# A one-core MoE and gated recurrence kernel: where its first zero stores, weight roundings, rank work and transposing loads stand

## The chip, the cores and the metric

The kernel runs on one core of a Trainium2 chip. The metric is the device time of one execution in microseconds (us). Three executions of the kernel before took 873.31, 873.27 and 871.41 us; their median is 873.27 us.

## The reference

The input `x` has 32 sequences of 256 tokens with 256 channels. Two layers follow each other, each with a residual sum:

```python
x = x + moe(x, cond, ...)              # shared expert + 2 of 8 routed experts per token
x = x + recurrence(cond, x, W, b, a)   # 256 steps over the tokens of a sequence
# moe, for every token:
shared = silu(xf @ w1) * (xf @ w3) @ w2
s = sigmoid(concat(xf, tf) @ router_W);  top 2 of s + router_bias;  gates = s_sel / sum(s_sel)
h = gelu(xf @ W1e[e]);  y = h @ W2e[e];  routed = sum of gate * y over the two experts
out = (shared + routed) / 3
# recurrence, for every step t:
gate = sigmoid(h @ Wh.T + z_t @ Wz.T + b);  h = tanh(h * (1 - alpha) + gate * z_t)
```

## The kernel before

Every float32 operand of a large product is split into two float16 parts, high and low, and three products (high by high, low by high, high by low) are summed. The split of a weight is called its rounding here. It takes one ScalarE operation (the high part, L1168) and one VectorE operation (the low part, L1482) on 128x1024 elements. `CONV` (L731 to L735) lists the eleven weight pieces in order: numbers 0 and 1 are w1 and w3, 2 is w2, 3 to 6 are the first expert matrices (w1e), 7 to 10 the second (w2e). `CONV_SLOT` says at which unit a piece is rounded; -1 is before the first unit. The pieces pass through four staging buffers, so the load of piece n waits until piece n-4 is rounded (L820).

The 8192 tokens are 64 tiles of 128 and lie in six sections of 8, 8, 12, 12, 12 and 12 tiles. A group is four tiles. A section passes through these steps:

- `load_x` (L795) loads a group of tokens on SP's queue. `x_high` on ScalarE and `low_x` on VectorE (L1020, L1213) split them into `x_parts`. `turn_x` (L807) then turns the group into `xs` with four transposing DMAs on SP's queue (L814).
- LOGITS: TensorE multiplies `xs` with the router weights. VectorE finds the two experts of each token in two parts of `route`. RANKS: TensorE counts the tokens of each expert. VectorE works out the slot of each token in `place`, again in two parts.
- `scatter` (L958) writes each tile twice into `x_slots` in device memory, one indirect DMA for each of its two experts, on GpSimd's queue. Slots that no token takes must hold zeros, so `clear_slots` (L932) stores zeros over all slots beforehand: 3 MB for the first section, 3 MB for the second, and later 1 MB each for the rows that the longer sections add.
- `load_pair` (L828) brings two tiles of slots back, turned, as `xe` (L834, SP's queue). There are four buffers for it.
- An expert unit computes the up product of one pair and the down product of the pair two units earlier. ScalarE evicts the result into `y_pair` (three buffers, L1055) and SP stores it (L851). `gather` (L971) fetches the two results of each token (L983, GpSimd's queue) and VectorE adds them with the gates (`gated`).
- A shared unit computes a part of the shared expert for one group.

The program is a list of 152 units in a fixed order. Section 0 has 8 shared units (0 to 7) and then 12 expert units (8 to 19). Section 1 has 12 expert units (20 to 31) and 8 shared units (32 to 39). Each later section has 16 expert units and 12 shared units. The 256 steps of the recurrence stand from unit 34 on, at places written out by hand in tables. Each engine has a function `body(u)`, and each walks through the same units in the same order. Each of the engines, and SP with its DMA issues, executes strictly in order. GpSimd starts what it has at unit u when the up products of the unit before have ended (L993).

`PREP_UNIT` gives the unit in which a group is split and turned: before, groups 2 and 3 at -1, groups 4, 5 and 6 (section 2) at 14, 16 and 18. `LOGITS_UNIT` was -3, 2, 21 for the first three sections, and RANKS came 3 units later for section 0 and 4 units later for the others. `SCATTER_AT` gives the units of the scatters: 2 to 6, 9 to 14 and 28 to 34 for the first three sections. The section's first slot loads wait for all its scatters: `first_pairs(0)` stands ahead of unit 0 on SP's queue, the wait for section 1 stands in unit 16 (L870), and `first_pairs(2)` in unit 35 (L881).

Of the kernel before, what the change touches and what calls it, by code (L numbers as in the profile page):

```python
# [71 lines left out]
LOGITS_UNIT = [-3, 2] + [START[_n - 1] + 1 for _n in range(2, NS)]  # L72
# [5 lines left out]
for _n in range(NS):  # L78
    _first = LOGITS_UNIT[_n] + 7
    _end = START[_n] - 5  # L80
    SCATTER_AT.append([2 + max(_j // 2, _j - 3) if _n == 0 else _first + min(_j, _j * max(_end - _first, 1) // SECTIONS[_n]) for _j in range(SECTIONS[_n])])
    _first = FIRST_PAIR[_n] + PAIRS[_n]
    GATHER_AT.append([_first + _j + (2 if _n == 0 else 1) for _j in range(SECTIONS[_n])])
# [318 lines left out]
for _n in range(NS):  # L402
    for _u, _what in ((0, LOGITS), (3 if _n == 0 else 4, RANKS)):
# [19 lines left out]
def moe_gated_recurrence(nc, x, cond, router_w, router_b, w1, w3, w2, w1e, w2e, gate_w, gate_b, alpha, out):  # L423
# [34 lines left out]
    with ExitStack() as ctx:  # L458
# [276 lines left out]
        CONV_SLOT = [-1] * NSTAGE + [0, 1, 2, 3, 4, 5, 6]  # L735
# [58 lines left out]
        def _(sp):  # L794
# [12 lines left out]
            def turn_x(q):  # L807
# [3 lines left out]
                for i in range(2):  # L811
                    sp.wait_ge(s_xlo, 2 * q + i + 1)
                    for j in (2 * i, 2 * i + 1):
                        sp.dma_start_transpose(xs[:, q % NXS].rearrange("p h k s -> p (h k) s")[:, :, j * P:(j + 1) * P],  # L814
                                               x_parts[:, q % NXP, j].rearrange("p h c -> p (h c)")).then_inc(s_xs[q % NXP], 16)
# [39 lines left out]
            def prepare(at):  # L855
                for q in range(N_GROUPS):
                    if PREP_UNIT[q] == at:
                        turn_x(q)
                        if q + NXT < N_GROUPS:
                            load_x(q + NXT)  # L860
# [51 lines left out]
        def _(pool):  # L912
# [92 lines left out]
        def _(act):  # L1005
# [175 lines left out]
            for q in range(TILE0[1] // GROUP):  # L1181
                for i in range(2):
                    x_high(q, i)
                if q < N_ACT_LOADS:
                    src, _, a, k, w = conv_parts(CONV[q])
# [634 lines left out]
```

## Time and profile before

| what | value |
|---|---|
| median of three runs | 873.27 us |
| span of the profiled execution | 964.0 us |
| TensorE busy (matmuls) | 771.4 us, 80% of the span |
| VectorE busy | 531.1 us, 55% |
| ScalarE busy | 461.6 us, 48% |
| GpSimd busy | 272.8 us, 28% |
| HBM read, written | 39.90 MB, 55.84 MB |

The profiled execution is one run of the program under the hardware profiler. Its own time is given as its span, 964.0 us from the first to the last instruction; no other time of that execution is recorded. It is 90.7 us longer than the median of the runs without the profiler. Durations below are from the profiled execution.

### The profile page before, as it was taken

The numbers are of one execution on the slowest core, as the hardware profiler recorded it, in microseconds if no ns is written. First come the engines' busy times: TensorE is split into PE (matmuls) and PEld (weight loads), VectorE is DVE, ScalarE is ACT, GpSimd is POOL, SyncE is SP. The second block draws the span as 40 slices with busy tenths as digits, with TensorE's granted clock in tenths as the row PEclk, the third lists the DMA queues.
The fourth block names the chain that finished last, engine by engine and source line by source line (L and its number), as shares of the span: only waits on it lengthen the run. The fifth ranks groups of instructions, "written<-read, shape, count | busy, mean of one in ns | idle before, by whom it ended". The sixth has DMA issues, their size and how long they took to land.

```text
span 964.0 us, 23915 instructions
## 1 busy us (share of the span) xinstructions
PE 771.4 (80%) x8642; PEld 547.5 (57%) x8642; DVE 531.1 (55%) x1974; ACT 461.6 (48%) x1332; POOL 272.8 (28%) x286
## 2 busy tenths in 40 slices
PE   2368857777999969998886999888698999998553
PEld 1135646643587735587763558675355887465332
DVE  4546413444766436758444777644477545677444
ACT  3345523243555534565552566555255666455233
POOL 2244403655203453401325330233432000432000
PEclk9679978798989998999998999989799999999555
DMA  7985999548637432955532484753253452222001
GB/s 194 364 257 121 210 206 216 168 148 178 156 85 188 137 116 72 208 110 140 161 116 88 97 189 78 157 125 127 77 121 88 90 139 98 90 72 66 1 12 45
DMA packets 180195, 127.99 MB, mean 133 GB/s; under 512 B 132434, under 2 KB 160884, under 8 KB 180084
## 3 DMA queue, kind: packets, MB, share of 16 engines
q1 hardware_dynamic: 164420, 83.39, 36.7%
q0 software_dynamic: 14400, 41.96, 13.8%
q8 instruction: 76, 1.25, 0.6%
q10 hardware_dynamic: 1264, 1.10, 0.5%
q14 instruction: 35, 0.29, 0.1%
HBM read 39.90 MB, written 55.84 MB: 99 GB/s over the span
## 4 chain that ended last, share of the span: by engine, by line
PE 52%; DVE 17%; ACT 10%; another core or an unknown queue 7%; issue 6%; SPq 4%; DMA 3%; DVEq 0%; ACTq 0%
PE bank L1550 51%; SPq L814 3%; DVE hid_low L1335 2%; DVE pre L1384 2%; DVE taken L1381 2%; ACT th L1093 2%; DMA y_got<-in_L_cond_W1e_dram 2%; DVE o_ch L1404 2%; ACT hs_high L1101 2%; DVE r_sum L1354 1%; PE bank L1722 1%; DVE r_part L1350 1%; ACT hid_high L1046 1%; DVE hs_low L1390 1%
## 5 line engine op out<-in xcount | busy, mean ns | idle before, releaser
L1550 PE MATMUL bank<-xe,w1e_high 128*128 128x128 f16 x1360 | 223.2, 227 | 22.4 <-DMA xe<-x_slots_even 7.1
L1550 PE MATMUL bank<-xs,w_high 128*128 128x512 f16 x512 | 176.3, 392 | 21.9 <-ACT full L1062 12.8
L1093 ACT ACTIVATE th<-bank 128x64 f32<-128x64 f32 x256 | 57.3, 224 | 226.7 <-PE bank L1550 171.0
L1335 DVE TENSOR_TENSOR hid_low<-full,hid_high 128x512 f16<-128x512 f32 (+1 forms) x152 | 103.0, 677 | 105.8 <-ACT hid_high L1046 75.3
L1550 PE MATMUL bank<-xe,w1e_low 128*128 128x128 f16 x680 | 150.7, 226 | 1.7 <-issue 1.6
L1381 DVE SCALAR_TENSOR_TENSOR taken<-th,zq 128x64 f32<-128x64 f32 x256 | 57.3, 224 | 171.2 <-ACT th L1093 151.6
L1550 PEld LDWEIGHTS bank<-xe,w1e_high 128*128 x1360 | 120.9, 101 | 42.0 <-issue 27.7
L1550 PE MATMUL bank<-hs_high,gwt_high 128*128 128x32 f16 x1024 | 80.4, 180 | 76.8 <-ACT hs_high L1101 63.3
L1550 PEld LDWEIGHTS bank<-hs_high,gwt_high 128*128 128x128 f16 x1024 | 69.6, 99 | 114.3 <-ACT hs_high L1101 84.0
L1101 ACT ACTIVATE hs_high<-pre 128x64 f16<-128x64 f32 x256 | 65.6, 256 | 99.3 <-DVE pre L1384 90.8
L1550 PE MATMUL bank<-xs,w_low 128*128 128x512 f16 x256 | 100.4, 392 | 0.3 <-issue 0.3
L1390 DVE TENSOR_TENSOR hs_low<-hist,hs_high 128x64 f16<-128x64 f32 x256 | 57.1, 223 | 77.6 <-ACT hist L1102 71.2
L1550 PE MATMUL bank<-w2e_high,hid_high 128*128 x340 | 97.3, 286 | 0.6 <-issue 0.5
L1550 PE MATMUL bank<-w2e_high,hid_low 128*128 x340 | 96.4, 283 | 1.6 <-issue 1.6
L1550 PEld LDWEIGHTS bank<-xs,w_high 128*128 128x128 f16 x512 | 51.1, 100 | 80.4 <-ACT full L1062 13.3
L1550 PE MATMUL bank<-w2e_low,hid_high 128*128 x340 | 96.1, 283 | 0.4 <-issue 0.4
L983 POOL DMA_INDIRECT y_got<-y_slots_odd,where x64 | 65.4, 1021 | 91.8 <-PE bank L1550 75.6
L953 POOL TENSOR_TENSOR fence_pool<-zero 128x1 f32<-128x1 f32 x12 | 3.7, 306 | 308.9 <-DMA y_slots_odd<-y_pair 92.2
L983 POOL DMA_INDIRECT y_got<-y_slots_even,where x64 | 65.1, 1018 | 81.8 <-PE bank L1550 63.2
L1042 ACT ACTIVATE full<-bank 128x512 f32<-128x512 f32 x88 | 50.8, 578 | 67.8 <-remote 41.2
L968 POOL DMA_INDIRECT x_slots_even<-x_parts,where x64 | 68.1, 1064 | 51.5 <-PE bank L1550 32.4
L968 POOL DMA_INDIRECT x_slots_odd<-x_parts,where x64 | 64.0, 1001 | 56.1 <-PE bank L1550 36.5
(152 smaller groups left out, 1746.1 us busy)
## 6 DMA issues: line engine op xcount, KB each, us to landing
y_slots_even<-y_pair SPq DMA_DIRECT2D x41, 256.0 KB
y_slots_odd<-y_pair SPq DMA_DIRECT2D x41, 256.0 KB
x_tok<-in_x_dram SPq DMA_DIRECT2D x16, 512.0 KB
x_res<-in_x_dram SPq DMA_DIRECT2D x16, 512.0 KB
out_dram<-o_tok SPq DMA_DIRECT2D x32, 256.0 KB
x_slots_even<-zeros POOLq DMA_DIRECT2D x1, 3072.0 KB, 16.1
x_slots_odd<-zeros POOLq DMA_DIRECT2D x1, 3072.0 KB, 23.5
y_got<-in_L_cond_W1e_dram SPq DMA_DIRECT2D x4, 512.0 KB, 20.3
```

What stands on the lines that cost most here:

```text
L814: sp.dma_start_transpose(xs[:, q % NXS].rearrange("p h k s -> p (h k) s")[:, :, j * P:(j + 1) * P], x_parts[:, q % NXP, j].rearrange("p h ...
L968: pool.indirect_dma_start(x_slots[n % 2], at_slots(n, j, k), x_parts[:, q % NXP, i].rearrange("p h c -> p (h c)"), None).then_inc(s_scat[n ...
L983: pool.indirect_dma_start(y_got[:, tile % NYG, k, :], None, y_slots[n % 2][0:(2 * PAIRS[n] - 1) * P, :], at_slots(n, j, k)).then_inc(s_got ...
L1042: nc.scalar.activation(full32[:, u.i % 2, 0:hidden(u)], up_bank(u)[:, 0:hidden(u)], ACT.Gelu, scale=1.0 / UP)
L1093: nc.scalar.activation(flat3(th[:, s % 2]), gate_sums(s), ACT.Tanh, scale=0.5 / UP).then_inc(s_th, 1)
L1101: nc.scalar.activation(flat3(hs[0][:, s % 2]), src, ACT.Tanh).then_inc(s_hhi, 1)
L1335: dve.tensor_tensor(hid[1][:, u.i % NR, some], full32[:, u.i % 2, some], hid[0][:, u.i % NR, some], ALU.subtract).then_inc(s_lo, 1)
L1381: dve.scalar_tensor_tensor(flat3(taken[:, s % 2]), flat3(th[:, s % 2]), 1.0, flat3(z_of(s // HALF)[:, s % HALF]), ALU.add, ALU.mult).then_ ...
L1384: dve.tensor_tensor(flat3(pre[:, s % 2]), flat3(taken[:, s % 2]), flat3(kept[:, s % 2]), ALU.add).then_inc(s_pre, 1)
L1390: dve.tensor_tensor(flat3(hs[1][:, s % 2]), flat3(hist[:, s % TS]), flat3(hs[0][:, s % 2]), ALU.subtract).then_inc(s_hlo, 1)
L1404: ins = dve.scalar_tensor_tensor(o_ch[:, kc].rearrange("p j b t -> p t j b"), z_of(c)[:, :, kc, :].rearrange("p (t j) b -> p t j b", j=2), ...
L1550: return pe.matmul(out_ap, w, mov, start=start, stop=stop, skip_group_check=True)
```

## The change

The zero store of section 0 is issued when the second group of tokens has landed (`s_x[1]`), and no longer when the first eight transposes are done. The zero store of section 1 waits until seven pieces (three shared and all of w1e) are rounded; it stands ahead of section 0's scatters on GpSimd. The load of w2 moves from SP's queue to ScalarE's. Pieces 3 to 6 are rounded at units 1, 1, 2, 2 and no longer at -1, 0, 1, 2; pieces 7 to 10 stay at 3, 4, 5, 6. SP loads four w1e pieces before it turns group 2, and a w2e piece between groups 2 and 3. Group 3 is split at unit 0. The logits of section 1 move from unit 2 to 4 with RANKS three units later, at 7 and not at 6; those of section 2 from unit 21 to 23 with RANKS at 27 and not at 25. Section 0's last scatter moves from unit 6 to 5, section 1's scatters lie one a unit at 9 to 16 and not at 9 to 14, and section 2's at 30 to 34 and not at 28 to 34. Section 2's groups are split at units 8, 12 and 18, and their twelve transposes are issued one a unit: at 8 to 11, 12 to 15 and 18 to 21.

```diff
-LOGITS_UNIT = [-3, 2] + [START[_n - 1] + 1 for _n in range(2, NS)]
+PREP_UNIT.update({3: 0, 4: 8, 5: 12, 6: 18})
+LOGITS_UNIT = [-3, 4, 23] + [START[_n - 1] + 1 for _n in range(3, NS)]
+RANKS_AFTER = [3, 3] + [4] * (NS - 2)
...
-    _first = LOGITS_UNIT[_n] + 7
+    _first = LOGITS_UNIT[_n] + RANKS_AFTER[_n] + (2 if _n == 1 else 3)
...
-        CONV_SLOT = [-1] * NSTAGE + [0, 1, 2, 3, 4, 5, 6]
+        CONV_SLOT = [-1] * N_SHARED_CONV + [1, 1, 2, 2, 3, 4, 5, 6]
...
-            def turn_x(q):
+            def turn_tile(q, j):
                 if q >= NXS:
                     sp.wait_ge(s_up, FIRST_SHARED[q - NXS] + MID)
-                for i in range(2):
-                    sp.wait_ge(s_xlo, 2 * q + i + 1)
-                    for j in (2 * i, 2 * i + 1):
-                        sp.dma_start_transpose(...)
+                sp.wait_ge(s_xlo, 2 * q + j // 2 + 1)
+                sp.dma_start_transpose(...)
...
             def prepare(at):
-                for q in range(N_GROUPS):
-                    if PREP_UNIT[q] == at:
-                        turn_x(q)
-                        if q + NXT < N_GROUPS:
-                            load_x(q + NXT)
+                for q in range(TILE0[2] // GROUP, N_GROUPS):
+                    spread = section_of(q * GROUP) == 2
+                    for j in range(GROUP):
+                        if PREP_UNIT[q] + (j if spread else 0) == at:
+                            turn_tile(q, j)
+                            if j == GROUP - 1 and q + NXT < N_GROUPS:
+                                load_x(q + NXT)
...
-            load_weight(N_ACT_LOADS)
             for q in range(TILE0[1] // GROUP):
                 load_x(q + NXT)
-            for n in range(N_ACT_LOADS + 1, NSTAGE + 2):
+            for n in range(N_SHARED_CONV, NSTAGE + 3):
                 load_weight(n)
-            for q in range(TILE0[1] // GROUP, N_GROUPS):
-                if PREP_UNIT[q] < 0:
-                    turn_x(q)
-                    if q + NXT < N_GROUPS:
-                        load_x(q + NXT)
-            for n in range(NSTAGE + 2, len(CONV)):
+            for q in range(TILE0[1] // GROUP, TILE0[2] // GROUP):
+                turn_x(q)
+                load_weight(NSTAGE + 1 + q)
+                load_x(q + NXT)
+            for n in range(NSTAGE + 5, len(CONV)):
                 load_weight(n)
...
-            for q in range(TILE0[1] // GROUP):
-                turned(pool, q)
+            pool.wait_ge(s_x[1], 16)
             pool.wait_ge(s_zero0, 2)
             clear_slots(0, 0, 0, PAIRS[0])
+            pool.wait_ge(s_conv, N_SHARED_CONV + 4)
             clear_slots(1, 1, 0, PAIRS[1])
...
-                if q < N_ACT_LOADS:
+                for n in (q, N_ACT_LOADS) if q == N_ACT_LOADS - 1 else (q,):
```

## Rows read from the trace of the kernel before

**Rows 1.** The page of the kernel before: its span.

```profile
span 964.0 us, 23915 instructions
```

**Rows 2.** Busy time by stretch; columns are in the header line.

```profile
core 0: us, PE busy (x) PEld busy (x) DVE busy (x) ACT busy (x) POOL busy (x), PEclk, DMA share, GB/s
24.00:48.00 24.00, 7.78 (x38) 2.89 (x37) 13.40 (x43) 7.13 (x11) 4.84 (x5) 0.64 1.01 364
48.00:72.00 24.00, 15.96 (x108) 7.24 (x106) 10.32 (x44) 10.41 (x14) 11.74 (x11) 0.79 0.90 258
120.00:144.00 24.00, 12.19 (x108) 10.34 (x109) 3.71 (x6) 5.99 (x13) 0.00 (x0) 0.78 1.04 210
400.00:500.00 100.00, 89.09 (x1212) 72.25 (x1211) 59.74 (x258) 58.41 (x174) 22.90 (x23) 0.95 0.54 139
```

**Rows 3.** SP's queue, timeline: start, duration, instruction, count.

```profile
6.58 10.52 SPq L814 DMA_TRANSPOSE xs<-x_parts  x8
...
19.67 11.60 SPq L823 DMA_DIRECT2D y_got<-in_L_cond_W1e_dram  x2
```

**Rows 4.** DMA issues, microseconds to landing last: zero stores of the first 150 us.

```profile
x_slots_even<-zeros POOLq DMA_DIRECT2D x1, 3072.0 KB, 16.1
x_slots_odd<-zeros POOLq DMA_DIRECT2D x1, 1024.0 KB, 14.2
```

**Rows 5.** Waits, 20 to 50 us: who waited for whom, total, times, longest.

```profile
PE bank L1550 <- ACT full L1062: 12.8, 1, 12.8
POOL fence_pool L953 <- DVE smask L1306: 20.6, 1, 20.6
```

**Rows 6.** TensorE timeline: the logits of section 1, with the wait ahead.

```profile
56.82 0.19 PE L1550 MATMUL bank<-rwx_high,xs 128*128 128x8 f16 x2 [7.46 <-DMA xs<-x_parts]
```

**Rows 7.** VectorE timeline, 25 to 45 us.

```profile
25.24 1.22 DVE L1482 SCALAR_TENSOR_TENSOR w_low<-y_got,w_high 128x1024 f16<-128x1024 f32 x1
...
37.65 0.23 DVE L1317 COPY ranks<-bank 128x72 f32<-128x72 f32 x1
...
42.15 2.49 DVE L1213 SCALAR_TENSOR_TENSOR x_parts<-x_tok,x_parts 128x512 f16<-128x512 f32 x4
44.55 0.68 DVE L1328 SCALAR_TENSOR_TENSOR full<-full,bank 128x512 f32<-128x512 f32 x1
```

**Rows 8.** GpSimd timeline: first, ninth and last scatter of section 0.

```profile
42.44 1.33 POOL L968 DMA_INDIRECT x_slots_even<-x_parts,where  x1 [0.33 <-issue]
...
64.15 1.31 POOL L968 DMA_INDIRECT x_slots_even<-x_parts,where  x1 [9.52 <-PE bank L1550]
...
74.01 1.22 POOL L968 DMA_INDIRECT x_slots_even<-x_parts,where  x1 [0.30 <-issue]
```

**Rows 9.** ScalarE timeline: first expert unit, three late evictions, unit 21.

```profile
84.54 0.60 ACT L1042 ACTIVATE full<-bank 128x512 f32<-128x512 f32 x1 [0.58 <-PE bank L1550]
...
129.81 0.60 ACT L1055 ACTIVATE y_pair<-bank 128x512 f32<-128x512 f32 x1 [9.68 <-DMA y_slots_even<-y_pair]
...
141.34 0.60 ACT L1055 ACTIVATE y_pair<-bank 128x512 f32<-128x512 f32 x1 [7.48 <-DMA y_slots_even<-y_pair]
...
146.40 0.60 ACT L1042 ACTIVATE full<-bank 128x512 f32<-128x512 f32 x1 [2.94 <-PE bank L1550]
...
151.69 0.38 ACT L1055 ACTIVATE y_pair<-bank 128x256 f32<-128x256 f32 x1 [4.21 <-DMA y_slots_even<-y_pair]
```

**Rows 10.** Chain of waits: one undisturbed expert unit of TensorE.

```profile
105.76 3.10 PE bank L1550 x36
```

**Rows 11.** SP's queue, timeline: the three groups of section 2.

```profile
112.40 11.66 SPq L814 DMA_TRANSPOSE xs<-x_parts  x4
...
129.42 5.20 SPq L814 DMA_TRANSPOSE xs<-x_parts  x4
...
141.35 5.14 SPq L814 DMA_TRANSPOSE xs<-x_parts  x4
```

**Rows 12.** Scatters of section 2 (L968): durations in ns, first and last start.

```profile
L968 POOL DMA_INDIRECT x_slots_even<-x_parts,where x24: 966/986/1439, 181.3 to 226.3; - x24
```

More of the change, by code:

```diff
@@ L78 @@
 for _n in range(NS):
-    _first = LOGITS_UNIT[_n] + 7
+    _first = LOGITS_UNIT[_n] + RANKS_AFTER[_n] + (2 if _n == 1 else 3)
     _end = START[_n] - 5
-    SCATTER_AT.append([2 + max(_j // 2, _j - 3) if _n == 0 else _first + min(_j, _j * max(_end - _first, 1) // SECTIONS[_n]) for _j in range(SECTIONS[_n])])
+    SCATTER_AT.append([2 + _j // 2 if _n == 0 else 9 + _j if _n == 1 else _first + min(_j, _j * max(_end - _first, 1) // SECTIONS[_n]) for _j in range(SECTIONS[_n])])
     _first = FIRST_PAIR[_n] + PAIRS[_n]
@@ L402 @@
 for _n in range(NS):
-    for _u, _what in ((0, LOGITS), (3 if _n == 0 else 4, RANKS)):
+    for _u, _what in ((0, LOGITS), (RANKS_AFTER[_n], RANKS)):
         _u += LOGITS_UNIT[_n]
@@ L805, in load_res, with turn_x @@
                 sp.dma_start(x_res[:].rearrange("p j c -> p (j c)"), x_in[q]).then_inc(s_res, 16)
-            def turn_x(q):
+            def turn_tile(q, j):
                 if q >= NXS:
                     sp.wait_ge(s_up, FIRST_SHARED[q - NXS] + MID)
-                for i in range(2):
-                    sp.wait_ge(s_xlo, 2 * q + i + 1)
-                    for j in (2 * i, 2 * i + 1):
-                        sp.dma_start_transpose(xs[:, q % NXS].rearrange("p h k s -> p (h k) s")[:, :, j * P:(j + 1) * P],
-                                               x_parts[:, q % NXP, j].rearrange("p h c -> p (h c)")).then_inc(s_xs[q % NXP], 16)
+                sp.wait_ge(s_xlo, 2 * q + j // 2 + 1)
+                sp.dma_start_transpose(xs[:, q % NXS].rearrange("p h k s -> p (h k) s")[:, :, j * P:(j + 1) * P],
+                                       x_parts[:, q % NXP, j].rearrange("p h c -> p (h c)")).then_inc(s_xs[q % NXP], 16)
+            def turn_x(q):
+                for j in range(GROUP):
+                    turn_tile(q, j)
             def load_weight(n):
@@ L855, in prepare @@
             def prepare(at):
-                for q in range(N_GROUPS):
-                    if PREP_UNIT[q] == at:
-                        turn_x(q)
-                        if q + NXT < N_GROUPS:
-                            load_x(q + NXT)
+                for q in range(TILE0[2] // GROUP, N_GROUPS):
+                    spread = section_of(q * GROUP) == 2
+                    for j in range(GROUP):
+                        if PREP_UNIT[q] + (j if spread else 0) == at:
+                            turn_tile(q, j)
+                            if j == GROUP - 1 and q + NXT < N_GROUPS:
+                                load_x(q + NXT)
             def body(u):
@@ L1183, in _ @@
                     x_high(q, i)
-                if q < N_ACT_LOADS:
-                    src, _, a, k, w = conv_parts(CONV[q])
-                    act.dma_start(stage[:, q].rearrange("p (k w) -> p k w", k=k), src).then_inc(s_stage[q], 16)
+                for n in (q, N_ACT_LOADS) if q == N_ACT_LOADS - 1 else (q,):
+                    src, _, a, k, w = conv_parts(CONV[n])
+                    act.dma_start(stage[:, n].rearrange("p (k w) -> p k w", k=k), src).then_inc(s_stage[n], 16)
             for n in range(N_ACT_LOADS):
@@ L1190, in _ @@
             act_sigmoid(0)
-            for n in range(N_ACT_LOADS, NSTAGE):
+            for n in range(N_ACT_LOADS, N_SHARED_CONV):
                 conv(n)
@@ L1464, in body @@
                         route(n, 6, N_ROUTE_LINKS, gap)
-                    if n > 0 and since == 4:
+                    if n > 0 and since == RANKS_AFTER[n]:
                         place(n, 0, 5, gap)
-                    if n > 0 and since == 5:
+                    if n > 0 and since == RANKS_AFTER[n] + 1:
                         place(n, 6, N_PLACE - 1, gap)
@@ L1534, in _ @@
             route(0, 0, N_ROUTE_LINKS, lambda: None)
-            for n in range(N_ACT_LOADS, NSTAGE):
+            for n in range(N_ACT_LOADS, N_SHARED_CONV):
                 conv(n)
```

## The prediction, made before the changed kernel ran

> **What bounds the kernel now.** I read the busy time by stretch first [rows 2]. From 400 to 500 us TensorE is busy for 89.09 of 100 us, so the late stages are bound by TensorE and the change touches nothing there. The early stretches differ. TensorE is busy for 7.78 of 24 us from 24 to 48 us, for 15.96 of 24 from 48 to 72, and for 12.19 of 24 from 120 to 144 us, while the DMA engines are at 0.90 to 1.04 of their time. The units stand in one fixed order, and each unit behind a late one is late too. I therefore count an early microsecond saved as one saved at the end.
>
> Then I read who waits in these stretches. In the first, TensorE waits 12.8 us for ScalarE's silu [rows 5], and ScalarE is late because it rounds a w1e piece whose load is slow. That load runs beside the 6 MB of zero stores: DMA moves 364 GB/s there [rows 2], and SP needs 11.60 us to issue two ordinary copies [rows 3]. VectorE is behind the same rounding, so the slots of section 0 come late and GpSimd waits 20.6 us for them [rows 5]. Next TensorE waits 7.46 us for the transposes of group 3 [rows 6]. GpSimd's scatters are held too: the ninth waits 9.52 us for TensorE's pace [rows 8]. In the third stretch ScalarE cannot evict because the store of an earlier result has not landed: 9.68, 7.48 and 4.21 us [rows 9]. Those stores are behind SP's twelve transposes for section 2, issued in three blocks of 11.66, 5.20 and 5.14 us [rows 11].
>
> **Part A, the start up to the first expert unit (unit 8).** Its up product ends at 84.54 us now [rows 9]. I follow the changed order from the end of the first eight transposes, which is 6.58 + 10.52 = 17.1 us [rows 3], plus a delay D, since the first zero store now runs beside them.
>
> - *D.* The trace shows no first-stage transpose beside a zero store. The nearest rows are the four of section 2 beside the later 1 MB stores (landing 14.2 us [rows 4]): 11.66 us, or 2.92 each, where the first eight take 10.52, or 1.32 each [rows 3, 11]. Eight at that price give D = 8 x 1.60 = 12.8 us. Below, D = 0 if the issue rate holds. By bytes alone, 3 MB at 364 GB/s [rows 2] are 8.6 us of all DMA engines, part of it in time that the transposes leave free. The rows where SP is slowed by zeros [rows 3, 11] are the nearest, so I take D = 6.
> - *VectorE to the last w1e piece.* Now the rounding of w2 ends at 25.24 + 1.22 = 26.46 us [rows 7], 9.4 us after the transposes; its load comes earlier on ScalarE's queue, which can't hold it longer. Behind it place(0) takes 42.15 - 37.65 = 4.5 us, with no slow load ahead of it any more. Group 2 takes half of 2.49, or 1.25 us, and group 3 the same in unit 0. Units 0 to 2 add three products and two low parts at 0.68 us and four roundings at 1.22 [rows 7], so 3.4 + 4.9 us. The sum is 17.1 + 9.4 + 4.5 + 2.5 + 8.3 = 41.8 us, plus D.
> - *GpSimd.* The wait for seven rounded pieces is new, and all sixteen scatters of section 0 are queued behind it, with whoever reads their slots. They start near 42.5 + D, where they start at 42.44 now [rows 8]. So VectorE's earlier place(0) is worth nothing by itself. What goes is the 9.52 us wait in their middle, because TensorE is ahead by then. Fifteen steps from the first to the last scatter take 74.01 - 42.44 - 9.52 = 22.05 us. The last one is issued 0.1 + D - 9.5 = D - 9.4 us later than now.
> - *Behind them.* The first pairs are loaded only when all scatters have landed, and from the last scatter to the end of the first expert unit I keep today's distance, 84.54 - 74.01 = 10.5 us [rows 8, 9]. The second 3 MB of zeros now runs beside the scatters, the w2e loads and group 3's transposes. It is bounded by 0 and by another 8.6 us; much of that traffic has slack, so I take 2 us.
> - Moving w2's load costs ScalarE one DMA issue and takes one from SP, and the logits of section 1 at unit 4 no longer meet an unfinished group 3, so I count nothing for either. If group 3 is still late there, its wait is a part of the 2 us.
>
> A comes to 9.4 - 6 - 2 = 1.4 us gained, between 9.4 and -12.
>
> **Part B, units 8 to 21.** ScalarE starts unit 21's eviction at 146.40 us, 61.9 us behind unit 8's [rows 9]. Thirteen undisturbed units of 3.10 us [rows 10] are 40.3 us, so 21.6 us are lost. The three waits for stores are 21.4 us of it [rows 9]. The change breaks the 22.0 us of blocks [rows 11] into single transposes, 1.3 us in a unit of 3.1. What comes in their place is the zero store of 2 MB at unit 16, not 14. In SP's order the wait for section 1's scatters stands in unit 16 as well, and behind it the slot loads, the stores and four transposes of group 6. With 2.92 us for a transpose, SP needs about 6.4 us for a unit of 3.1 over the 14.2 us of the zeros [rows 4, 10, 11], so it slips by 7 to 8 us. The last scatter, issued only in unit 16, adds about 2 us. Three y_pair buffers and four slot buffers swallow a part of this, but I charge 10 of the 21.4 us and take 11 us gained. Ends: 3 us if the waits only change their place, 18 us if the buffers cover nearly all.
>
> **Part C, section 2's scatters.** GpSimd spends 24 x (0.986 + 0.30) = 30.9 us on them, from 181.3 to 226.3 us [rows 8, 12], and the gathers of section 1 are queued in between. Now they start two units later, 6.2 us [rows 10]. The stretch also holds eight gathers of about the same cost, 10 us, and spans 46.3 us, so some 5 us of it are slack. The last scatter comes 1 to 6 us later, and TensorE's residual products of section 1 wait for the gathers behind it. I take 2 us lost, between 0 and 6. The ranks and the router work are as many instructions as before and I count nothing for their new places; they are a few short VectorE operations ahead of nothing that is late.
>
> **The sum.** 1.4 + 11 - 2 = 10.4 us gained, 953.6 us against the profiled 964.0 [rows 1]. The median of the runs is 873.27, or 0.906 of the profile. Scaled by that the gain is 9.4 us, and the time is 864.
>
> **Rivals.**
>
> *The zeros do not slow the transposes.* D = 0, and the slip in part B goes too, from 10 to about 5 us. For it: in the trace sixteen of the transposes [rows 3, 11] take about 1.3 us each, beside other traffic. Against it: the rows with zeros in flight [rows 3, 11]. The gain is 7.4 + 16 - 2 = 21 us in the profile, but the start can't gain it all, since TensorE's shared units need their time; with half of the start's part, 17 us. The time is 873.3 - 15.5 = 858. The Trainium skill (DMA: Bandwidth & Descriptors, section Queues, rings and completion order) says that each DMA engine takes turns between its queue rows, a whole packet at a time, so that GpSimd's zeros could not shut SP's row out. By that rule D would be small, which is this rival. The trace speaks against it for SP's copies, with 11.60 us for issuing two [rows 3].
>
> *The zero stores hold SP, twice (slower).* D = 12.8 at the start, and the 2 MB at unit 16 now meets the slot loads on which the change from section 0 to section 1 hangs. The start is 9.4 - 12.8 - 2 = -5.4 us, B keeps 3 us, C costs 6: together 8.4 us lost, or 881 us. The point from which this decides is the first block of eight: if it takes longer than 10.5 + 9.4 = 20 us, the start loses. For it: the 2.92 us for each transpose [rows 11]. Against it: one 3 MB store may be done before the eight are.
>
> *It does not spread what matters (no change).* The late evictions wait for the landing of a store, and DMA is at 1.04 from 120 to 144 us [rows 2]. If the DMA engines and not SP's order hold the stores, spreading the issues changes nothing: B gives 3 us and C takes 2, the start 1.4, for about 871 us. Against it: the DMA load falls by the time of section 2's zeros alone, and the waits stand exactly behind the blocks.
>
> **How the numbers follow.** My chances are 0.44 for the forecast (864, own range 857 to 869), 0.20 for no slowing by zeros (858), 0.18 for the slower case (881) and 0.18 for no change (871). The range from 852 to 878 takes in the first two and the last, and leaves out the upper half of the slower case and the far end of the best. Some 0.3%, or 2.6 us, is what a measurement of this kernel can tell from no change. The first two cases and a small part of the no-change case are faster by more: 0.66. Within it: 0.16. Slower by more: 0.18.
>
> **What would show it.** Right for the start: the first eight transposes take 14 to 19 us where they take 10.5 now, the 12.8 and 9.52 us waits are gone, the first scatter is issued near 48 us and section 0's scatters show no gap. Right for part B: from unit 8 to unit 21 it takes about 51 us and not 61.9, with waits for y_pair below 10 us in all. Right for part C: GpSimd's scatters of section 2 stand back to back to their end. The prediction is wrong if the eight transposes keep 10.5 us or take over 20, if the scatters start before 42 us, or if large waits for stores come back beside the zeros of unit 16.

## Result and profile after

The kernel after takes 876.81 us (median of 20 runs, 874.2 to 879.64) against 874.18 us (20 runs, 870.98 to 879.04) for the kernel before on the same chip. The ratio is 1.0028, 95% interval 1.0017 to 1.0039: it is slower by 2.5 us. The forecast was 864 us and faster, so its direction was wrong, though 876.8 lies inside the stated 852 to 878.

The span of the kernel after's profiled execution stands where its runs do:

```profile
span 876.0 us, 23945 instructions
```

Busy time by stretch in the kernel after (columns in the header line, as in [rows 2]):

```profile
core 0: us, PE busy (x) PEld busy (x) DVE busy (x) ACT busy (x) POOL busy (x), PEclk, DMA share, GB/s
24.00:48.00 24.00, 13.70 (x99) 6.16 (x100) 16.10 (x75) 8.79 (x13) 0.00 (x0) 0.87 0.75 184
48.00:72.00 24.00, 18.98 (x122) 8.47 (x120) 11.30 (x28) 10.54 (x14) 15.08 (x15) 0.93 0.99 334
120.00:144.00 24.00, 19.59 (x249) 16.45 (x248) 5.09 (x8) 10.66 (x21) 0.00 (x0) 0.79 1.07 220
400.00:500.00 100.00, 95.68 (x1128) 68.34 (x1126) 68.56 (x246) 59.00 (x189) 44.98 (x46) 1.00 0.59 154
```

From 24 to 48 us TensorE is busy for 13.70 us, where [rows 2] have 7.78; from 48 to 72 us for 18.98 and not 15.96; from 120 to 144 us for 19.59 and not 12.19. The early stretches look as well as they were forecast. The comparison is not fair, though. The profiled execution of the kernel before, 964.0 us [rows 1], was an odd one. A second one of the very same kernel (the first experiment) has the span below. What made the first one long stays open.

```profile
span 873.2 us, 23915 instructions
```

From here on, the kernel before means this second execution. ScalarE evicts the up product of a unit when it is done. The starts of these evictions give the progress of four of the kernels, in us. This table is read off ScalarE's timelines:

```
unit   first trace of before   before, 2nd    after   section 2 undone
  0            38.5                36.8        35.5        35.9
  3            63.9                63.8        52.7        53.1
  5            72.4                72.3        68.5        67.6
  8            84.5                84.5        84.8        85.7
 21           146.4               137.2       132.3       139.8
 23           158.5               148.6       138.6       151.2
 24           160.0               150.1       148.5       153.3
 28           184.3               165.1       164.6       167.7
 36           239.2               203.3       203.3       205.0
 37           244.1               211.9       215.1       213.9
151           876.3               785.1       788.3       788.9
```

The whole course can be read here. Against the second trace of before, the kernel after is 11 us ahead at unit 3 and level at unit 8. It is 10 us ahead at unit 23 and level at unit 28. At unit 37 it is 3.2 us behind, and at unit 151 still 3.2 us: from unit 37 to unit 151 both take 573.2 us. So two leads came and went, and one loss stayed.

*The first lead.* SP's queue and the landing of the two zero stores in the kernel after (us last):

```profile
6.82 21.00 SPq L816 DMA_TRANSPOSE xs<-x_parts  x8
```

```profile
x_slots_even<-zeros POOLq DMA_DIRECT2D x1, 3072.0 KB, 18.3
x_slots_odd<-zeros POOLq DMA_DIRECT2D x1, 3072.0 KB, 13.8
```

The first eight transposes take 21.00 us, against 10.52 in [rows 3]: the first zero store runs beside them and costs 10.5 us. GpSimd's queue in the kernel after shows the second store, then the first and the last scatter of section 0:

```profile
7.04 1.24 POOL L942 DMA_DIRECT2D x_slots_even<-zeros  x1 [3.60 <-DMA x_tok<-in_x_dram]
...
53.07 1.06 POOL L942 DMA_DIRECT2D x_slots_odd<-zeros  x1 [44.79 <-DVE w1e_low L1489]
...
54.53 1.92 POOL L975 DMA_INDIRECT x_slots_even<-x_parts,where  x1 [0.18 <-issue]
...
76.06 0.97 POOL L975 DMA_INDIRECT x_slots_even<-x_parts,where  x1 [0.30 <-issue]
```

The first scatter is at 54.53 us and not 42.44 [rows 8], the last at 76.06 and not 74.01. The pause amid the scatters is gone, as forecast, and it paid for the later start and no more. Waits from 20 to 90 us (total, times, longest):

```profile
PE bank L1557 <- DMA xs<-x_parts: 22.5, 1, 22.5
ACT w2e_high L1175 <- DMA y_got<-in_L_cond_W2e_dram: 10.5, 2, 9.9
```

TensorE waits 22.5 us for its first transposes. Most of the lead of unit 3 is lost at unit 5: ScalarE waits 9.9 us for a w2e piece, whose load now runs beside the second zero store. The rest is lost up to unit 8. There TensorE waits for ScalarE, which is late because of that piece, and its granted clock is lower. TensorE's waits from 60 to 86 us in the kernel after, then the stretch from unit 5 to unit 8 in the kernel after and in the second trace of before:

```profile
PE bank L1557 <- ACT full L1069: 4.9, 1, 4.9
PE bank L1557 <- ACT zq L1089: 2.7, 1, 2.7
```

```profile
68.50:84.80 16.30, 12.88 (x78) 5.92 (x78) 13.38 (x58) 11.86 (x17) 7.01 (x6) 0.79 0.75 226
```

```profile
72.30:84.50 12.20, 12.12 (x89) 6.34 (x86) 11.72 (x39) 7.87 (x12) 2.23 (x3) 1.00 0.54 120
```

No wait of TensorE for `xe` stands among them. So by these traces unit 8 of the kernel after hung on the late weight piece and the clock, and not on the scatters.

*The second lead.* ScalarE waited for stores of y_pair from 84 to 150 us for 18.5 us in the kernel before and 10.6 us in the kernel after:

```profile
ACT y_pair L1055 <- DMA y_slots_even<-y_pair: 18.5, 4, 7.5
```

```profile
ACT y_pair L1062 <- DMA y_slots_even<-y_pair: 10.6, 6, 6.0
```

ScalarE's evictions of units 8, 21 and 24 in the kernel after:

```profile
84.78 0.60 ACT L1049 ACTIVATE full<-bank 128x512 f32<-128x512 f32 x1 [1.05 <-PE bank L1557]
...
132.33 0.60 ACT L1049 ACTIVATE full<-bank 128x512 f32<-128x512 f32 x1 [0.96 <-PE bank L1557]
...
148.51 0.60 ACT L1049 ACTIVATE full<-bank 128x512 f32<-128x512 f32 x1 [7.22 <-PE bank L1557]
```

Units 8 to 21 take 47.5 us, against 61.9 in [rows 9] but 52.7 in the second trace of before. Unit 24 then waits 7.22 us for TensorE, which does the logits only now and has waited 3.5 us for group 6's last transpose. So of the 10.0 us at unit 23, 4.9 were there at unit 21, and the other 5.1 are the logits put off (units 21 to 23 take 11.4 us before and 6.3 after). The 4.9 us are gone at unit 29 (173.4 against 173.5). In between TensorE waits longer than in the kernel before in three places: 3.5 against 0.9 us for that transpose, 2.8 against 2.2 for `hid_low`, behind the route work on VectorE, and 2.3 against 1.4 for the residual sums, behind place on VectorE. Together that is 4.1 us.

*The loss that stayed.* GpSimd's queue at the first scatter of section 2, in the kernel after and in the second trace of before:

```profile
173.46 0.19 POOL L960 TENSOR_TENSOR fence_pool<-zero 128x1 f32<-128x1 f32 x1 [6.31 <-PE bank L1557]
173.81 1.01 POOL L975 DMA_INDIRECT x_slots_even<-x_parts,where  x1 [0.15 <-issue]
```

```profile
167.02 0.33 POOL L953 TENSOR_TENSOR fence_pool<-zero 128x1 f32<-128x1 f32 x1
167.51 1.19 POOL L968 DMA_INDIRECT x_slots_even<-x_parts,where  x1 [0.16 <-issue]
```

The scatters start 6.3 us later. From the first to the last of them GpSimd is never idle for more than the 0.3 us between two issues, in either trace. The last one starts at 209.71 us after and 206.54 before. ScalarE waits for it: `x_high` for the next group writes a buffer of `x_parts` that section 2's scatters read, and it stands in program order ahead of ScalarE's next recurrence step. The last scatter and `x_high`, after and then before:

```profile
209.71 0.97 POOL L975 DMA_INDIRECT x_slots_even<-x_parts,where  x1 [0.30 <-issue]
212.23 0.63 ACT L1027 ACTIVATE x_parts<-x_tok 128x512 f16<-128x512 f32 x1 [8.43 <-issue]
```

```profile
206.54 0.98 POOL L968 DMA_INDIRECT x_slots_even<-x_parts,where  x1 [0.30 <-issue]
209.06 0.63 ACT L1020 ACTIVATE x_parts<-x_tok 128x512 f16<-128x512 f32 x1 [5.13 <-issue]
```

VectorE's next step waits for ScalarE, `r_sum` is behind it, and TensorE's residual products (the fp32 products with `r_sum`) wait for that, after and before:

```profile
213.94 1.22 PE L1557 MATMUL bank<-ident_keep,r_sum 128*128 128x128 f32 x4 [5.25 <-DVE r_sum L1361]
```

```profile
210.77 0.71 PE L1550 MATMUL bank<-ident_keep,r_sum 128*128 128x128 f32 x4 [1.96 <-DVE r_sum L1354]
```

In the traces of the twelve experiments and of the kernel after, `x_high` starts 2.51 to 2.53 us behind the last scatter's start and unit 37 another 2.8 us behind that. The end of section 2's scatters on GpSimd's queue, not a gather, releases unit 37.

### The profile page after: what moved, and what is told of

Its sections match the earlier page's. It is cut to its first block, busy times and chain, and to the rows that moved or that the text cites. A ratio compares the mean times of both kernels' runs of the same rounds, so it can differ in the third digit from the quotient of the medians.

```text
span 876.0 us, 23945 instructions
## 1 busy us (share of the span) xinstructions
PE 744.1 (85%) x8642; PEld 539.6 (62%) x8642; DVE 530.5 (61%) x1974; ACT 461.5 (53%) x1332; POOL 271.7 (31%) x286
## 4 chain that ended last, share of the span: by engine, by line
PE 53%; DVE 18%; ACT 9%; DMA 6%; issue 6%; POOL 5%; SPq 2%; DVEq 0%; ACTq 0%; POOLq 0%
PE bank L1557 51%; POOL x_slots_even L975 3%; DVE o_ch L1411 3%; SPq L816 2%; DVE taken L1388 2%; DVE pre L1391 2%; DVE hid_low L1342 2%; DMA y_got<-in_L_cond_W2e_dram 2%; DMA xe<-x_slots_even 2%; ACT th L1100 2%; ACT hs_high L1108 2%; PE bank L1729 1%; POOL y_got L990 1%; DVE r_part L1357 1%; DVE r_sum L1361 1%
## 5 line engine op out<-in xcount | busy, mean ns | idle before, releaser
L1557 PE MATMUL bank<-xe,w1e_high 128*128 128x128 f16 x1360 | 217.0, 222 | 10.5 <-DVE hid_low L1342 3.9
L1557 PE MATMUL bank<-xs,w_high 128*128 128x512 f16 x512 | 176.2, 393 | 10.6 <-DVE full L1335 5.1
L1557 PE MATMUL bank<-xe,w1e_low 128*128 128x128 f16 x680 | 147.7, 222 | 0.0
L1557 PEld LDWEIGHTS bank<-xe,w1e_high 128*128 x1360 | 117.3, 99 | 28.8 <-issue 15.7
L1557 PE MATMUL bank<-hs_high,gwt_high 128*128 128x32 f16 x1024 | 79.7, 179 | 43.2 <-ACT hs_high L1108 42.3
L1397 DVE TENSOR_TENSOR hs_low<-hist,hs_high 128x64 f16<-128x64 f32 x256 | 57.0, 223 | 77.2 <-ACT hist L1109 75.7
L1557 PE MATMUL bank<-w2e_high,hid_high 128*128 x340 | 95.2, 280 | 0.0
L1557 PE MATMUL bank<-w2e_high,hid_low 128*128 x340 | 94.4, 278 | 0.0
L975 POOL DMA_INDIRECT x_slots_odd<-x_parts,where x64 | 65.3, 1020 | 41.2 <-PE bank L1557 25.4
L1557 PE MATMUL bank<-hs_high,gwt_low 128*128 128x32 f16 x1024 | 77.8, 178 | 0.0
```

The source lines that it names most:

```text
L975: pool.indirect_dma_start(x_slots[n % 2], at_slots(n, j, k), x_parts[:, q % NXP, i].rearrange("p h c -> p (h c)"), None).then_inc(s_scat[n ...
L1397: dve.tensor_tensor(flat3(hs[1][:, s % 2]), flat3(hist[:, s % TS]), flat3(hs[0][:, s % 2]), ALU.subtract).then_inc(s_hlo, 1)
L1557: return pe.matmul(out_ap, w, mov, start=start, stop=stop, skip_group_check=True)
```

## Experiments

Times are medians, and ratios are against the kernel before on the same chip with 95% intervals. For every profile I also give U8 and U37, the starts of units 8 and 37, and S2, the first scatter of section 2. A profile is one execution, and some lie off their medians: those of experiments 2, 3 and 6 are 4 us longer than the median of their runs, that of experiment 11 is 4 us shorter. So times compare by the ratios, and the profiles serve to show who waits for whom.

**1. The kernel before, profiled again** (no edit).

> The kernel before, unchanged, profiled once more. The profiled execution of the kernel after has a span of 876.0 us, right at its median of 876.8, while the one of before had 964.0 us against 874.2. Theory O (the 964 us execution was an odd one): the span is now 870 to 880 us, and some of the waits on which the forecast rested (the y_pair waits of 21.4 us, the 9.5 us wait amid the scatters) are smaller. Theory P (profiling lengthens the kernel before and not the one after): 955 to 970 us again.

The span is 873.2 us, so theory O holds: the 964.0 us were one odd execution. Its waits for y_pair are 18.5 us and not 21.4, so those waits are real. Units 3, 5 and 8 come at the same time to 0.1 us (unit 0 is 1.7 us earlier). The stages behind unit 8 were too long by about 90 us in all, and units 8 to 21 by 9.2 us of that.

**2. The first zero store back behind the eight transposes.**

```diff
-            pool.wait_ge(s_x[1], 16)
+            for q in range(TILE0[1] // GROUP):
+                turned(pool, q)
```

> The kernel after, with the first zero store again behind the first eight transposes. Theory A (the zero store lengthens those eight from 10.5 to 21.0 us and everything behind is late by that): the transposes take 10.5 us, the first scatter is issued near 45 us and not 54.5, unit 8 comes 8 to 10 us earlier, and the time is 866 to 869 us, faster than both. Theory B (the delay is swallowed before the end, because the scatters, the second zero store or a later stage set the pace): 874 to 877 us.

877.5 us, 1.0033 (1.0017 to 1.0049). Theory A's mechanism holds and its time does not. SP's and GpSimd's queues show the transposes, both zero stores, and the first scatter; then ScalarE's waits for w2e loads from 28 to 75 us:

```profile
6.72 11.74 SPq L816 DMA_TRANSPOSE xs<-x_parts  x8
...
20.33 1.24 POOL L942 DMA_DIRECT2D x_slots_even<-zeros  x1 [16.89 <-issue]
...
43.75 1.07 POOL L942 DMA_DIRECT2D x_slots_odd<-zeros  x1 [22.18 <-DVE w1e_low L1490]
...
45.22 1.07 POOL L976 DMA_INDIRECT x_slots_even<-x_parts,where  x1 [0.18 <-issue]
```

```profile
ACT w2e_high L1176 <- DMA y_got<-in_L_cond_W2e_dram: 20.0, 2, 18.5
```

The transposes take 11.74 us and the first scatter is at 45.22 us, 9.3 us earlier than in the kernel after. Unit 3 begins at 43.4 us and not 52.7. Then ScalarE waits 18.5 us for one w2e piece, whose load runs beside the second zero store, which comes earlier too. In experiment 11, where that store is moved away, the longest such wait is 5.7 us. Unit 5 begins at 72.2 us and U8 is 87.1. Theory B holds: the second store takes all of it back. U37 is 218.2.

**3. Section 2 undone.**

```diff
-PREP_UNIT.update({3: 0, 4: 8, 5: 12, 6: 18})
-LOGITS_UNIT = [-3, 4, 23] + [START[_n - 1] + 1 for _n in range(3, NS)]
+PREP_UNIT.update({3: 0})
+LOGITS_UNIT = [-3, 4] + [START[_n - 1] + 1 for _n in range(2, NS)]
...
-                    spread = section_of(q * GROUP) == 2
+                    spread = False
```

> The kernel after, with section 2 as before: its groups split and turned in blocks at units 14, 16, 18, its logits at 21, its scatters from 28. Theory A (the spread transposes save about 10 us between units 8 and 21): 884 to 888 us. Theory C (in an ordinary execution the blocks cost little, and the later scatters of section 2 take back what is left): 874 to 878 us. Theory D (the section 2 part itself makes the kernel after slow): below 872 us.

874.72 us, 0.9993 (0.9977 to 1.0009), the same as the kernel before and the lower edge of theory C. Theory A is excluded. So all that the change does to the start comes to nothing, and the section 2 part is what makes the kernel after slower. In the traces the section 2 part is ahead by 3.1 us at unit 28 (164.6 against 167.7), of which 0.9 us were there at unit 8, and loses 4.2 us up to unit 37 (U37 215.1 against 213.9).

**4. Only the section 2 part, in the kernel before** (its edits as in the diff of the change).

> The kernel before, with the section 2 part of the change alone. Theory A: 862 to 866 us. Theory C: 872 to 877 us. Theory D: above 878 us.

877.22 us, 1.0032 (1.0016 to 1.0049): on the border between theories C and D, and far from A. From both sides the section 2 part costs 2.1 to 3 us. ScalarE's waits for y_pair from 84 to 150 us fall to 8.7 us here, and are 20.6 us in experiment 3, so it is the spread transposes that remove them. U8 is 83.1, S2 173.7, U37 214.9.

**5. The kernel after, section 2's scatters from unit 29.**

```diff
-    _first = LOGITS_UNIT[_n] + RANKS_AFTER[_n] + (2 if _n == 1 else 3)
+    _first = LOGITS_UNIT[_n] + RANKS_AFTER[_n] + (2 if _n in (1, 2) else 3)
```

> The kernel after, with section 2's scatters from unit 29 and not 30. In the traces the kernel after holds a lead of 10 us at unit 23, none at unit 28, and from unit 37 on it is 3.2 us behind. Theory Q (GpSimd's queue sets unit 37: the scatters of section 2 stand back to back, the gathers of section 1 are behind them, and in the kernel after GpSimd idles 6.3 us ahead of unit 30): that idle time goes, unit 37 comes 3 to 5 us earlier, and the time is 871 to 874 us. Theory R (the spread transposes or the later logits cost the time in another place): 876 to 878 us, as the kernel after.

876.97 us, 1.0024 (1.0006 to 1.0042): theory R's time. GpSimd's queue shows why:

```profile
171.86 0.21 POOL L960 TENSOR_TENSOR fence_pool<-zero 128x1 f32<-128x1 f32 x1 [3.33 <-issue]
172.56 1.01 POOL L975 DMA_INDIRECT x_slots_even<-x_parts,where  x1 [0.49 <-issue]
```

The scatters still start at 172.56 us. They wait now for VectorE's place, not for TensorE's pace. Its last slots, in this kernel:

```profile
171.23 0.17 DVE L1309 TENSOR_SCALAR where<-low_slot 128x12 int32<-128x12 f32 x1
```

VectorE's timeline in the kernel after and in the kernel before, from the ranks' copy to the last step of place:

```profile
164.43 0.26 DVE L1324 COPY ranks<-bank 128x104 f32<-128x104 f32 x1
...
171.68 0.24 DVE L1315 TENSOR_REDUCE gate<-smask 128x12 f32<-128x96 f32 x1
```

```profile
157.12 0.26 DVE L1317 COPY ranks<-bank 128x104 f32<-128x104 f32 x1
...
163.50 0.24 DVE L1308 TENSOR_REDUCE gate<-smask 128x12 f32<-128x96 f32 x1
```

Place ends at 171.9 us in the kernel after and at 163.7 in the kernel before. The later logits moved it into units 27 and 28, where it shares VectorE with the residual sums of section 0. Unit 37 comes at 213.8 us, 1.2 us earlier than in the kernel after, as S2 does; the timed runs cannot tell that from nothing.

**6. The kernel before, section 2's scatters from unit 30.**

```diff
-    _first = LOGITS_UNIT[_n] + 7
+    _first = LOGITS_UNIT[_n] + (9 if _n == 2 else 7)
```

> The kernel before, with nothing changed but section 2's scatters from unit 30 and not 28. Theory Q: 877 to 880 us, as slow as the kernel after or slower, from unit 37 on. Theory R: 874 to 875 us, as the kernel before.

877.45 us, 1.0028 (1.0012 to 1.0044): theory Q. This one number, without any other edit, makes the kernel as slow as the whole change does. GpSimd idles as in the kernel after:

```profile
176.04 0.19 POOL L953 TENSOR_TENSOR fence_pool<-zero 128x1 f32<-128x1 f32 x1 [5.58 <-PE bank L1550]
```

S2 is 176.4 and U37 217.7.

**7. The kernel before, its second zero store behind section 0's last scatter.**

```diff
             clear_slots(0, 0, 0, PAIRS[0])
-            clear_slots(1, 1, 0, PAIRS[1])
...
+                if u.i == max(SCATTER_AT[0]):
+                    clear_slots(1, 1, 0, PAIRS[1])
                 if u.i == max(SCATTER_AT[1]):
```

> The kernel before, with the 3 MB zero store of section 1 issued behind the last scatter of section 0 (unit 6) and not together with section 0's at 19 us. Theory V (the start is bound by what the DMA engines must move before the last w2e pieces and section 0's scatters are through, 0.93 of their time up to 68 us, so a store that can wait should wait): the w1e pieces land some 8 us earlier, unit 8 comes 6 to 10 us earlier, and if no later stage takes it back the time is 865 to 869 us. Theory W (GpSimd's and SP's order sets the pace further on, and takes an early gain back by unit 28): 872 to 876 us, though unit 8 is early.

880.26 us, 1.0059 (1.0036 to 1.0082): neither theory, slower. Unit 3 begins at 64.0 us as before. The wait that ends there is for the last w1e piece. Its load stands behind eight transposes in SP's queue, which wait for VectorE and start no earlier without the store (42.35 us, against 41.18 in the second trace of before). The store now falls on the first slot loads (GpSimd's queue, and TensorE's wait for `xe` from 76 to 92 us, both of this kernel):

```profile
75.32 1.07 POOL L935 DMA_DIRECT2D x_slots_odd<-zeros  x1
```

```profile
PE bank L1551 <- DMA xe<-x_slots_even: 4.0, 1, 4.0
```

U8 is 90.9 us and not 84.5. U37 is 220.0.

**8. The kernel after with both zero stores moved, and scatters from unit 29** (the edits of 2, 5 and 10 together).

> The kernel after, with the first zero store behind the first eight transposes, the second behind the last scatter of section 0 (unit 5), and section 2's scatters from unit 29. Theory V with Q: transposes at 10.5 to 12 us, first scatter at 44 us, unit 8 at 74 to 77 us and not 84.8, and the time is 862 to 867 us. Theory W: 871 to 875 us.

866.84 us, 0.9916 (0.9891 to 0.9941), faster than both kernels. U8 is 77.2, S2 164.4, U37 205.9. Moving the same store cost 0.6% in the kernel before and helps here. With the order of the change the scatters are through 14 us earlier (the store is issued at 61.3 us, and at 75.3 in experiment 7). It does run beside the first slot loads here too: SP's first five take 15.6 us, against 7.5 in the kernel after. But they begin at 62.8 us, and no wait of TensorE for `xe` stands ahead of unit 8.

**9. The kernel after, section 2's RANKS at unit 26 and scatters from 28.**

```diff
-RANKS_AFTER = [3, 3] + [4] * (NS - 2)
+RANKS_AFTER = [3, 3, 3] + [4] * (NS - 3)
...
-    _first = LOGITS_UNIT[_n] + RANKS_AFTER[_n] + (2 if _n == 1 else 3)
+    _first = LOGITS_UNIT[_n] + RANKS_AFTER[_n] + (2 if _n in (1, 2) else 3)
```

> The kernel after, with section 2's RANKS at unit 26 and its scatters from unit 28. In five traces unit 37 begins 41.6 to 42.3 us behind the first scatter of section 2 wherever these scatters start late. Moving only the scatters (from 30 to 29) started them 1.6 us earlier, because VectorE's place for section 2 ended at 171.1 us, in units 27 and 28, where it shares VectorE with the residual sums of section 0. Theory Q: with place in units 26 and 27 the first scatter comes at 166 to 168 us and not 173.8, unit 37 at 209 to 212 us, and the time is 871 to 874 us. Theory R (the lead from the spread transposes is lost elsewhere and the scatters' start is not what sets unit 37): 876 to 878 us.

873.61 us, 0.9983 (0.9968 to 0.9998): theory Q's time, and with it the loss of the change is gone. (Counted as here, the distance of 41.6 to 42.3 us in the expectation is 41.2 to 41.5.) The trace is nearer to the kernel after than I expected. The first scatter is at 169.94 us:

```profile
169.94 1.00 POOL L975 DMA_INDIRECT x_slots_even<-x_parts,where  x1 [0.49 <-issue]
```

U37 is 214.5, not 209 to 212. At unit 29 this profile is 4.4 us later than the kernel after: TensorE waits 4.0 us there for the residual sums of section 0, behind the second part of place on VectorE, where the kernel after waits 2.3. Of the profiled executions only one stands for each kernel, and differences of 1 or 2 us between two of them do not carry a verdict. The timed runs do.

**10. The kernel after, only the second zero store moved.**

```diff
-            pool.wait_ge(s_conv, N_SHARED_CONV + 4)
-            clear_slots(1, 1, 0, PAIRS[1])
...
+                if u.i == max(SCATTER_AT[0]):
+                    clear_slots(1, 1, 0, PAIRS[1])
```

The edit also takes away the wait for seven rounded pieces, which held the scatters.

> The kernel after, with only the second zero store moved: behind section 0's last scatter (unit 5) and not ahead of the first. The first store stays beside the first eight transposes. Theory V (the second store delays the w2e loads and the scatters, the first the transposes, and each is paid for): transposes still take 20 to 21 us, the wait of 9.9 us for a w2e piece goes, section 0's scatters start at about 45 us, unit 8 comes at 78 to 81 us, and the time is 870 to 873 us. Theory X (one store beside loads is as good as the other; only their sum of bytes ahead of the scatters counts): unit 8 at 84 us, 876 to 878 us.

873.42 us, 0.9975 (0.9957 to 0.9994): theory V, 0.4 us above its range. SP's transposes and GpSimd's first scatter, then ScalarE's wait for w2e loads:

```profile
6.66 20.59 SPq L816 DMA_TRANSPOSE xs<-x_parts  x8
...
41.33 1.30 POOL L973 DMA_INDIRECT x_slots_even<-x_parts,where  x1 [0.54 <-issue]
```

```profile
ACT w2e_high L1175 <- DMA y_got<-in_L_cond_W2e_dram: 2.7, 1, 2.7
```

The transposes keep 20.59 us, the scatters start at 41.33 us and the wait for w2e falls from 10.5 to 2.7 us. U8 is 80.1, U37 211.0. That the scatters start earlier comes from the wait that is gone, and the shorter wait for w2e from the store that is gone. No run moves the one without the other, so how the gain divides between them is not shown.

**11. The kernel after, both zero stores moved, section 2 as it is.**

> The kernel after, with both zero stores moved (the first behind the first eight transposes, the second behind section 0's last scatter) and nothing else; section 2 as in the kernel after. Theory V: unit 8 at 77 us, 867 to 869 us, so that the zero stores alone account for all of the 7 to 10 us between the kernel after and the version with scatters from unit 29. If it is above 872 us, the start at unit 29 was worth most of it.

867.94 us, 0.9932 (0.9909 to 0.9955): theory V. SP's transposes and the first scatter:

```profile
6.79 10.97 SPq L816 DMA_TRANSPOSE xs<-x_parts  x8
...
37.19 1.04 POOL L974 DMA_INDIRECT x_slots_even<-x_parts,where  x1 [0.19 <-issue]
```

U8 is 75.6, S2 163.4, U37 204.4. The first store by itself was worth nothing (experiment 2); with the second one out of the way it is worth the step from 873.42 to 867.94 us (ratios 0.9975 and 0.9932, whose intervals just fail to overlap).

**12. Both zero stores moved, RANKS at 26, scatters from 28.**

> Both zero stores moved, and section 2's RANKS at unit 26 with its scatters from 28. Theories V and Q together: unit 8 at 77 us, first scatter of section 2 at 158 to 160 us, unit 37 at 201 to 203 us, 862 to 865 us. Theory R: 866 to 868 us, as without the earlier RANKS.

867.4 us, 0.9912 (0.989 to 0.9934). By the median this is theory R; by its ratio it can't be told from experiments 8 and 11, whose intervals overlap with it. Its profile has U8 at 80.1 us and not 77, and U37 at 206.8, so the expected 201 to 203 was missed too. What the earlier RANKS add on top of the moved stores stays open.

## Why the prediction was wrong, step by step

*The profiled execution taken as typical.* The page gave 964.0 us beside 873.27 us of the runs, 10% more, and I scaled by 0.906 where I should have asked which stages were long. From unit 8 to unit 21 the excess was 9.2 us (61.9 against 52.7), from unit 28 to unit 29 alone 3.2 us. Part A is untouched by this. Part B is not: an ordinary execution loses 52.7 - 40.3 = 12.4 us there and not 21.6, so 11 us would have been nearly all of it.

*Part A, D.* I took 6 us; the trace shows 10.5, and the bound of 12.8 from the transposes of section 2 [rows 11] was nearly met. It is also over the 20 us that the prediction named as a sign of being wrong. The rest of the chain held: 41.8 + 10.5 = 52.3 us for the last w1e piece, and GpSimd, released by it, issues its store at 53.07; the last scatter at 75.1 by the same sum, 76.06 measured. The step behind it, today's distance of 10.5 us from the last scatter to unit 8, did not hold: it is 8.7 us, since TensorE did not wait for the slots.

*Part A, the 2 us for the second store.* This term was mis-sized. The wait for the w2e piece is 9.9 us in the kernel after and 18.5 in experiment 2, and moving that store, with the wait ahead of it, gives 3.4 us by medians and 0.5% by ratios (experiment 10). Of the lead of 11.1 us at unit 3, 3.8 are left at unit 5 and none at unit 8. In all, the start lost 0.3 us at unit 8 where I had 1.4 gained. Experiment 3 confirms nothing gained to the end (0.9993).

*Part B.* Spreading the blocks did what was forecast at its place: the waits for y_pair fell from 18.5 to 10.6 us. Units 8 to 21 take 5.2 us less, half of the 11. The reading itself had a slip: the third of the three waits, 4.21 us, ends at 151.69 us, behind unit 21's eviction at 146.40, so only 17.2 us lie in the stretch, and that they nearly made up the lost 21.6 was chance. The step that failed is the first one of the whole argument: "I therefore count an early microsecond saved as one saved at the end". The 4.9 us of unit 21 are gone at unit 29, most of them in the waits listed above. Behind that, GpSimd's queue sets the time of unit 37. A lead that unit 8 has does reach the end, if section 2's scatters come earlier with it: in experiment 11 U8 is 9.2 us earlier than in the kernel after, S2 10.4, U37 10.6, and the time is 8.9 us shorter.

*Part C.* I wrote "The ranks and the router work are as many instructions as before and I count nothing for their new places". They were not free. Route and place in their new units are 1.5 of the 4.1 us of waits above, and place ends 8.2 us later than before. In the kernel after itself it does not hold the scatters: they wait 6.31 us for TensorE's pace, that is for unit 30. It does hold them in experiment 5, so moving them one unit up brought nothing. With RANKS and scatters both earlier the loss is gone (experiment 9, 0.9983). The price for the later scatters, 2 us of 0 to 6, was right in its range: experiment 6 measures 3.2 us by medians, 0.28% by ratio. But I set it against a gain of 11 us, of which nothing was left when the scatters began, and so the price stood alone. Over eight profiles with scatters from unit 29 or 30, U37 is 41 us behind S2:

```
                   S2      U37    U37 - S2
after             173.8   215.1    41.3
section 2 only    173.7   214.9    41.2
scatters from 29  172.6   213.8    41.2
before, from 30   176.4   217.7    41.3
experiment 2      176.9   218.2    41.3
experiment 8      164.4   205.9    41.5
experiment 10     170.1   211.0    40.9
experiment 11     163.4   204.4    41.0
before            167.5   211.9    44.4
section 2 undone  170.1   213.9    43.8
experiment 7      175.3   220.0    44.7
experiment 9      169.9   214.5    44.6
experiment 12     162.3   206.8    44.5
```

With scatters from unit 28 it is 43.8 to 44.7 us. That is not slack, of which the forecast had 5 us: GpSimd's queue is full from the first to the last scatter in all thirteen, with four to six gathers between, where the forecast had eight. Most of the difference is two gathers of section 0, 2.6 us, which fall between the scatters when these start at unit 28 and ahead of the first one otherwise. The last scatter comes 3.2 us later in the kernel after, half of the 6.3 us of the first. Six of the eight start with unit 30, so their distance could as well be TensorE's pace; in experiments 5 and 8 they start by place, and it is the same 41 us. Where the queue starts is set by the gathers of section 0 ahead, by TensorE's pace or by place, whichever is last.

*The rivals.* The slower one was right about the first zero store and named the wrong place for the second harm. It was decided not by SP's order at unit 16 but by GpSimd's queue at unit 30. The one of no change, that the DMA engines and not SP's order hold the stores, does not fit: the waits for y_pair fell, though the DMA share from 120 to 144 us is 1.07 and was 1.04. The rival that zeros do not slow the transposes is excluded for the first store: 19.9 to 21.2 us in the five traces with the store beside them, 10.5 to 12.0 us in the nine without. In the Trainium skill (DMA: Bandwidth & Descriptors, section Queues, rings and completion order) the engines take turns between queue rows packet by packet. The prediction's rival drew from it that little delay was to be expected, which the rule does not say: if two rows with work take equal turns, each has half of them. That agrees with the transposes, which kept half their rate beside the store, but no run here tests it against another way of sharing.

*The range.* That 876.8 us lies in 852 to 878 says nothing for the sum. The upper end was there for the case of no change, which expected 871 us for another reason.

*What stays open.* That the lead of unit 21 goes into the three waits listed is read from two traces; no run moved the logits of section 2 by themselves. What the wait for seven rounded pieces costs without the store behind it was not tried, and why the first execution was long is not known.

## What to carry to other kernels

A gain ahead of a full queue is worth only what reaches that queue's start: find the last fully used queue (here GpSimd's, from section 2's first to its last scatter), find who waits for its end (here ScalarE, for a buffer that the scatters read), and ask of each edit when it lets that queue begin. A bulk store that nobody needs soon belongs where no load that an engine waits for runs beside it; moving one of two such stores may show nothing while the other still costs as much. When the profiled span is 10% over the runs, profile once more before building a sum on it.

## What the runs showed of the hardware

- A 3 MB store of 128 partitions from GpSimd's queue took 11.6 to 18.6 us to land beside other traffic, and the second of two issued together 23.4 to 24.1 us. Beside it eight SBUF-to-SBUF transposing DMAs on SP's queue took 21.00 us, against 10.54 without it. ScalarE waited up to 18.5 us for a 512 KB load that ran beside one (experiment 2), and up to 5.7 us with the store moved (experiment 11).
- An indirect DMA of 128 rows on GpSimd's queue mostly took 0.97 to 1.03 us, and 0.30 us passed to the next. ScalarE, which waited for the last scatter before it wrote the same buffer, went on 2.5 us after that scatter had started.
- The same program gave profiled spans of 964.0 and 873.2 us, while 20 timed runs of it lay between 870.98 and 879.04 us. In the long execution TensorE's granted clock was 0.897 against 0.919 on average.
